# Cross-attention with chunks in twos: weighted sums of two chunks after each even chunk, two projection pieces after each odd chunk

## The chip, the cores and the metric

The kernel runs on one core of one Trainium2 chip. The metric is the device time of one execution in microseconds (us). A core has five engines that run side by side and wait for each other through semaphores: TensorE (PE, matrix products; the loading of its stationary operand is listed apart as PEld), VectorE (DVE), ScalarE (ACT), GpSimd (POOL) and SyncE (SP), which issues the transfers.

## The reference, cut to what matters

A decoder layer on 8 sequences of 512 rows and 256 features: a retention layer, a cross-attention and a mixture-of-experts layer. Only the cross-attention is touched by the change.

```python
# x: (8, 512, 256) after the retention layer, context: (8, 1601, 256), 16 heads of 16
xn = layernorm(x)
q, k, v = xn @ Wq.T + bq, context @ Wk.T + bk, context @ Wv.T + bv      # split into 16 heads
scores = einsum('bhtd,bhcd->bhtc', q, k) / sqrt(16)
out = einsum('bhtc,bhcd->bhtd', softmax(scores, axis=-1), v)
x = x + out.reshape(B, T, D) @ Wo.T + bo
```

## The kernel before, in words

The three layers follow each other. In the cross-attention, each of the 8 batches goes through 4 groups of 4 heads (`g`), and each group through 13 chunks of 128 context rows (`c`; the last has 65 rows). So a batch has 52 chunks. The programs of the engines are written out by hand; nothing reorders them. A chunk consists of these steps:

- **Scores** (line 964): four products of 128 context rows with 512 query rows, one for each head. Heads stand in pairs: one of a pair in partitions 0 to 63, the other in 64 to 127, so that a product uses half of the array's rows. The results go to three banks of PSUM in turn (`S_BANKS`), so that the fourth score of a chunk has to wait until ScalarE has taken the exponential of the first.
- **Exponentials** (line 1060, ScalarE): four per chunk, from PSUM into `x_probs`, with 8 slots before (two chunks).
- **Weighted sums** (line 948, `values`): four products of `x_probs` with the values, one for each head, each in 32 columns of the array, which accumulate over the chunks into one bank of PSUM, `PV`. In the trace each of the four shows as two records, so x8 is one chunk. They are run one chunk late. At the end of a group ScalarE copies the bank out (`evacuate`, line 1043), and the next group's first weighted sums wait for that.
- **Maxima** (line 900 on TensorE, line 1155 on VectorE; the last 66 columns are the "tails", lines 860 and 1159): the softmax subtracts each row's maximum, which has to be known before the group starts. So the scores of the next group are computed once more ahead of time, in another layout, and VectorE reduces them. About four of them belong to each chunk. Like the scores they use half of the array's rows, and a maximum and a score that stand next to each other and use different halves run together.
- **Pieces**: all other products, one after another in a table. For the next batch: 4 pieces of the projection `q` (line 879), 14 of `k` (line 886), 13 of `v` (line 893), 2 transposes `xnT` (line 873). For this one: `norm` (line 920, a group's result turned, then divided by VectorE), `oT` (line 924) and `wo` (line 931, the output projection), and `shift` (line 915, the maxima turned into rows). A `q`, `k` or `v` piece shows in the trace as x4, a `wo` piece as x8, in full array width and height. ScalarE takes `q`, `k`, `v`, `xnT`, `oT` and `shift` out of PSUM, VectorE the others.

Maxima and pieces share four banks of PSUM in turn (`W_BANKS`); each waits for what was four places ahead of it to be taken out. `woven` writes the scores of one pair of heads with the maxima around them: one maximum, the two scores, one maximum. `pieces_of` sets which piece stands in which chunk. TensorE's order in a chunk before is: two scores with two maxima, the piece (if there is one), two scores with two maxima, the weighted sums of the chunk before. In batches with a batch before and behind, 45 of 52 chunks have a piece; the seven without are chunks 0, 1 and 3 of group 0 and chunks 8, 9, 11 and 12 of group 3.

Of the kernel before, what the change touches and what calls it, by code (L numbers as in the profile page):

```python
# [23 lines left out]
P = 128  # L24
B, T, D, H = 8, 512, 256, 16
# [521 lines left out]
SPLITS = KT * NQ + KT * NK  # L547
WHOLE = 4
AHEAD = 4
NORM_CHUNK, SHIFT_CHUNK = 2, SC - 3  # L550
NEGM_AT = 320
# [24 lines left out]
def pieces_of(prev, following):  # L576

    at = [[[] for _ in range(SC)] for _ in range(G)]

    def spread(g, chunks, items):  # L580
        for c, item in zip(chunks, items):
            at[g][c].append(item)

    others = [c for c in range(SC) if c not in (NORM_CHUNK, SHIFT_CHUNK)]
    if prev:
        spread(0, (NORM_CHUNK, 4, 5, 7, 8), [("norm", G - 1), ("oT", 0), ("oT", 1), ("wo", 0), ("wo", 1)])
    for g in range(1, G):
        at[g][NORM_CHUNK].append(("norm", g - 1))
    for g in range(G):
        if g < G - 1 or following:  # L590
            at[g][SHIFT_CHUNK].append(("shift", (g + 1) % G))
    if following:
        q, k, v = q_pieces(), [k_pieces(f) for f in range(KT)], v_pieces()
        spread(0, (6, 9, 11, 12), [v[0], ("xnT", 0), ("xnT", 1), q[0]])
        spread(1, others, q[1:4] + k[0] + v[1:2])
        spread(2, others, k[1] + v[2:6])
        spread(3, others, v[6:13])
    return at


def work_of(prev, following):
# [21 lines left out]
    pieces = pieces_of(prev, following)  # L623
    return [[(first[g][c], pieces[g][c], second[g][c]) for c in range(SC)] for g in range(G)]

# [74 lines left out]
def cross_attention(nc, x_all, ln2, io, given):  # L700

    with ExitStack() as ctx:
# [21 lines left out]
        zero = sb("x_zero", [P, 1])  # L724
        probs = sb("x_probs", [P, 2 * GH, T])
        ou = sb("x_ou", [P, T])
# [127 lines left out]
        def _(pe):  # L854
# [80 lines left out]
            def values(b, g, q):  # L935

                if q == 0:
                    if b or g:
                        pe.wait_ge(pv_evac, b * G + g)
                    else:  # L940
                        pe.wait_ge(pv_zeroed, 1)
                    pe.wait_ge(v_ready, b * 2 * G + 2 * (g + 1))
                x = b * CHUNKS + g * SC + q
                pe.wait_ge(exp_done, GH * (x + 1))
                w = min(P, S - q * P)
                for j in range(GH):
                    slot = (GH * x + issued(j)) % (2 * GH)
                    m = pe.matmul(ps[32 * j:32 * j + HD + 1, PV, :], vst[g][0:w, q, j, :],  # L948
                                  probs[0:w, slot, :], start=q == 0, stop=q == SC - 1)
                m.then_inc(pv_used, 1)  # L950
# [30 lines left out]
            for b in range(B):  # L981
                for g in range(G):
                    pe.wait_ge(m_loaded, MLOADS * (b * G + g + 1))
                    for c in range(SC):
                        first, pieces, second = PLANS[b][g][c]
                        n = woven(b, g, c, 0, n, first)
                        for i in range(len(pieces)):
                            fill(b, n + i, g)
                        n = woven(b, g, c, 1, n + len(pieces), second)
                        if c:  # L990
                            values(b, g, c - 1)
                        elif b or g:
                            values(b - (g == 0), (g - 1) % G, SC - 1)
# [6 lines left out]
        def _(act):  # L1000
# [49 lines left out]
            for b in range(B):  # L1050
                for g in range(G):
                    for c in range(SC):
                        w = min(P, S - c * P)
                        for pair in range(2):
                            x = b * CHUNKS + g * SC + c
                            for s in range(GH * x + 2 * pair, GH * x + 2 * pair + 2):
                                act.wait_ge(s_filled, s + 1)
                                if x >= 2:
                                    act.wait_ge(pv_used, x - 1)
                                nc.scalar.activation(probs[0:w, s % (2 * GH), :], ps[0:w, s % S_BANKS, :],  # L1060
                                                     ACT.Exp, scale=HD ** -0.5).then_inc(exp_done, 1)
                            if c == 1 and pair == 0 and (b or g):

                                if b and g == 0:
                                    act.wait_ge(drained_v, done(b - 1, ("norm", G - 2)))
                                elif b and g == 1:
                                    act.wait_ge(drained_v, done(b, ("norm", G - 1)))
                                elif g >= 2:
                                    act.wait_ge(drained_v, done(b, ("norm", g - 2)))
                                evacuate(b * G + g)  # L1070
                            for item in [item for part in PLANS[b][g][c][2 * pair:2 * pair + 2] for item in part]:
                                if item[0] in BY_ACT:
                                    drain(b, n, g)
                                n += 1
            act.wait_ge(drained_v, done(B - 1, ("norm", G - 2)))
# [55 lines left out]
        def _(dve):  # L1131
# [75 lines left out]
            for b in range(B):  # L1207
                for g in range(G):
                    for c in range(SC):
                        if g == 0 and c == 7 and b < B - 1:  # L1210
                            dve.wait_ge(drained_a, done(b, ("oT", 1)) if b else done(LEADER, ("xnT", 1)))
                            normalise(b + 1)
# [566 lines left out]
```

## Time and profile before

| | us |
|---|---|
| median of 3 runs | 2213.64 (2205.82 to 2221.99) |
| the profiled execution, its own time | 2199.31 |
| its span, first to last instruction | 2197.5 |
| TensorE busy | 2041.6 (93%) |
| VectorE busy | 1523.5 (69%) |
| ScalarE busy | 1226.0 (56%) |
| GpSimd busy | 439.9 (20%) |

The cross-attention takes about 1330 us of the span, from some 430 us to some 1770 us. The time between two evacuations of `PV`, which are 13 chunks apart, is the period of a group. The end of a matmul in the trace is modelled, so the starts are what is read here: the distance from the start of one kind of work to the start of the next one is what the first kind costs TensorE.

### The profile page before, as it was taken

Reading aid. Unit: us, or ns where it says so; the run is one execution under the profiler, and the core shown is the slowest. Engines: PE = TensorE matmul, PEld = TensorE weight load, DVE = VectorE, ACT = ScalarE, POOL = GpSimd, SP = SyncE. Lnnn points to the kernel's source line nnn. Section 1 sums busy time; section 2 is a strip of 40 time slices with the busy share of each in tenths; the row PEclk is TensorE's granted clock in tenths of the full one; section 3 lists DMA queues with packets and bytes.
Section 4 is the critical chain, followed back from the end, with each engine's and each line's share of the span. In section 5 each row is a group of like instructions: output and inputs, shape, how many; then the busy total and the mean of one; then the engine's idle time right before and its main releaser. Section 6 shows DMA issues by size and latency. Waiting matters only on the chain. (4 is left out here: it accounts for less than half of the span.)

```text
span 2197.5 us, 36726 instructions
## 1 busy us (share of the span) xinstructions
PE 2041.6 (93%) x12946; PEld 1114.6 (51%) x12946; DVE 1523.5 (69%) x2930; ACT 1226.0 (56%) x2353; POOL 439.9 (20%) x484
## 2 busy tenths in 40 slices
PE   6898895899999999999999999999999879799999
PEld 4665664434444444444444434444433258588887
DVE  6888884677777787787787787787789266522222
ACT  2311312167767777777777777777777733222222
POOL 1100102203103112113113113112110044222222
PEclk9999997589989999999999999999999979899999
DMA  5000003434322522522521621621620010000000
GB/s 174 1 0 0 0 1 80 81 73 94 77 61 76 94 61 71 99 61 70 101 61 64 106 61 58 113 61 57 114 31 2 1 63 17 1 10 19 10 19 19
DMA packets 45373, 118.69 MB, mean 54 GB/s; under 512 B 9120, under 2 KB 21408, under 8 KB 45088
## 3 DMA queue, kind: packets, MB, share of 16 engines
q1 hardware_dynamic: 45232, 116.88, 23.7%
q8 instruction: 80, 1.31, 0.3%
q14 instruction: 61, 0.50, 0.1%
HBM read 77.30 MB, written 38.81 MB: 53 GB/s over the span
## 5 line engine op out<-in xcount | busy, mean ns | idle before, releaser
L1155 DVE TENSOR_REDUCE x_mx<-x_ps 128x1 f32<-128x512 f32 x1536 | 976.1, 685 | 217.2 <-PE x_ps L900 208.1
L1060 ACT ACTIVATE x_probs<-x_ps 128x512 f32<-128x512 f32 (+1 forms) x1664 | 894.3, 597 | 280.6 <-PE x_ps L964 274.6
L964 PE MATMUL x_ps<-x_qst,x_kst 50*128 50x512 f32 (+1 forms) x1664 | 595.6, 453 | 24.2 <-ACT x_probs L1060 22.1
L900 PE MATMUL x_ps<-x_kst,x_qst 48*128 48x512 f32 x1536 | 574.6, 462 | 16.8 <-DMA x_kst<-k_parts 11.1
L900 PEld LDWEIGHTS x_ps<-x_kst,x_qst 48*128 48x128 f32 x1536 | 240.3, 191 | 434.1 <-DVE x_mx L1155 289.2
L948 PE MATMUL x_ps<-x_probs,x_vst 128*17 128x512 f32 (+1 forms) x3328 | 446.2, 608 | 4.8 <-ACT x_ou L1043 4.8
L964 PEld LDWEIGHTS x_ps<-x_qst,x_kst 50*128 50x128 f32 (+1 forms) x1664 | 243.0, 183 | 116.4 <-ACT x_probs L1060 111.0
L1582 DVE TENSOR_TENSOR f_hid_whole<-f_ps,f_act_g 128x512 f32<-128x512 f32 x80 | 55.1, 690 | 240.8 <-PE f_ps L1339 232.2
L1454 ACT ACTIVATE f_act_g<-f_ps 128x512 f32<-128x512 f32 x80 | 47.6, 596 | 243.9 <-PE f_ps L1370 232.0
L1520 POOL TENSOR_TENSOR f_hid_rest<-f_hid_whole,f_hid_rounded 128x512 fp32r<-128x512 f32 x80 | 103.1, 1289 | 233.2 <-ACT f_hid_rounded L1460 233.2
L1092 POOL TENSOR_TENSOR x_vst<-x_v_all,x_bv 128x768 f32<-128x768 f32 x64 | 66.5, 1068 | 379.1 <-ACT x_v_all L1018 300.4
L284 ACT ACTIVATE r_qwide<-r_qT,r_headmask 128x512 f32<-128x512 f32 x128 | 80.0, 709 | 105.0 <-DVE r_qT L433 105.0
L213 PE MATMUL r_ps<-r_qwide,r_kT 128*128 128x512 f32 x256 | 116.2, 602 | 10.0 <-DVE r_vz L439 10.0
L948 PEld LDWEIGHTS x_ps<-x_probs,x_vst 128*17 128x17 f32 (+1 forms) x3328 | 55.3, 95 | 136.8 <-issue 73.3
L886 PE MATMUL x_ps<-x_ctxT,x_wk 128*128 128x256 f32 (+1 forms) x448 | 123.5, 402 | 0.0
L893 PE MATMUL x_ps<-x_wv,x_ctxT 128*128 128x256 f32 (+1 forms) x416 | 114.9, 404 | 4.0 <-DMA x_ctxT<-in_ctxT 4.0
L756 POOL TENSOR_TENSOR x_kp<-x_rest,x_zero 128x256 fp32r<-128x256 f32 (+1 forms) x105 | 59.4, 566 | 287.7 <-ACT x_rest L1038 234.4
L886 PEld LDWEIGHTS x_ps<-x_ctxT,x_wk 128*128 128x128 f32 x448 | 77.3, 197 | 45.2 <-issue 28.3
L448 DVE TENSOR_TENSOR r_probs<-r_ps,r_decay 128x512 f32<-128x512 f32 x128 | 84.5, 688 | 22.2 <-PE r_ps L213 21.4
L1384 PE MATMUL f_ps<-f_wd_rounded,f_hid_rest 128*128 128x256 f32 x320 | 91.9, 287 | 8.6 <-issue 4.6
L893 PEld LDWEIGHTS x_ps<-x_wv,x_ctxT 128*128 128x128 f32 (+1 forms) x416 | 70.3, 186 | 45.2 <-issue 25.1
L1384 PE MATMUL f_ps<-f_wd_rounded,f_hid_rounded 128*128 128x256 f32 x320 | 91.6, 286 | 0.0
(191 smaller groups left out, 2487.1 us busy)
## 6 DMA issues: line engine op xcount, KB each, us to landing
x_kst<-k_parts SPq DMA_DIRECT2D x192, 200.1 KB, 8.4
k_parts<-x_kp SPq DMA_DIRECT2D x16, 1601.0 KB, 6.0
x_ctxT<-in_ctxT SPq DMA_DIRECT2D x8, 1601.0 KB, 8.6
x_qst<-q_parts SPq DMA_DIRECT2D x192, 64.0 KB, 2.6
q_parts<-x_qp SPq DMA_DIRECT2D x8, 1024.0 KB, 4.3
x_all<-in_x SPq DMA_DIRECT2D x8, 512.0 KB, 3.9
out<-x_all SPq DMA_DIRECT2D x8, 512.0 KB, 2.9
x_qst<-x_mrows SPq DMA_DIRECT2D x128, 4.0 KB
```

The lines of the kernel that those rows point to most:

```text
L213: pe.matmul(ps[:, o, :], kT[:, f, c * P:(c + 1) * P], qwide[:, f, 4 * half:4 * half + 4, c * P:(c + 1) * P], start=True, stop=True).then_i ...
L284: ins = nc.scalar.activation(qwide[:, f, h, :], qT[:, f, :], ACT.Copy, scale=headmask[:, h:h + 1])
L448: nc.vector.tensor_tensor(probs[:, c % 2, h:h + 4, :], ps[:, item(), :].rearrange("p (h t) -> p h t", h=4), decay[:, h:h + 4, :], ALU.mult ...
L886: m = pe.matmul(o[:, 0:w], wk[:, kk, f * P:(f + 1) * P], ctxT[:, kk, c:c + w], start=kk == 0, stop=kk == KT - 1)
L893: m = pe.matmul(o[0:w, 0:D], ctxT[:, kk, c * P:c * P + w], wv[:, kk, :], start=kk == 0, stop=kk == KT - 1)
L900: m = pe.matmul(o, qst[mg][rows, pair, t * P:(t + 1) * P], kst[mg][rows, pair, i * 512:(i + 1) * 512], start=True, stop=True)
L948: m = pe.matmul(ps[32 * j:32 * j + HD + 1, PV, :], vst[g][0:w, q, j, :], probs[0:w, slot, :], start=q == 0, stop=q == SC - 1)
L964: pe.matmul(ps[0:w, n % S_BANKS, :], kst[g][rows, pair, c * P:c * P + w], qst[g][rows, pair, :], start=True, stop=True).then_inc(s_filled, 1)
L1060: nc.scalar.activation(probs[0:w, s % (2 * GH), :], ps[0:w, s % S_BANKS, :], ACT.Exp, scale=HD ** -0.5).then_inc(exp_done, 1)
L1155: nc.vector.tensor_reduce(out=mx[:, 2 * pair + half, t, i:i + 1], in_=o, axis=AX.X, op=ALU.max).then_inc(drained_v, 1)
L1384: m = pe.matmul(ps[:, DOWN + t // 2, (t % 2) * D:(t % 2 + 1) * D], hid[l][:, buf, t * P:(t + 1) * P], wd[r][:, j, :], start=start and n == ...
L1520: nc.gpsimd.tensor_tensor(hid[1][:, buf, :], hid_whole[:, buf, :], hid[0][:, buf, :], ALU.subtract).then_inc(hid_split, 1)
```

## The change

- Within a chunk all four scores now come first, with the maxima around them, and then either the piece(s) or the weighted sums, never both.
- Chunks 2, 4, ..., 12 of a group end with the weighted sums of the two chunks before them, eight products in a row. Chunk 0 ends with those of the last chunk of the group before. Odd chunks have none.
- Pieces stand in chunks 1, 3, 5, 7, 9 and 11 alone, mostly two in a row.
- `x_probs` has 12 slots in place of 8 (three chunks), `x_rest`, through which `q` and `k` pieces go to be split, has 2 in place of 4.
- ScalarE copies `PV` out after the exponentials of chunk 0 instead of in the middle of chunk 1. It takes pieces out after all four exponentials of a chunk. `normalise` for the next batch moves from chunk 7 to 5, `shift` from chunk 10 to 9, `norm` from chunk 2 to 1.

```diff
-WHOLE = 4
+WHOLE = 2
+SLOTS = 3 * GH
 AHEAD = 4
-NORM_CHUNK, SHIFT_CHUNK = 2, SC - 3
+VISITS = range(1, SC - 1, 2)
+NORM_CHUNK, SHIFT_CHUNK = VISITS[0], VISITS[4]
...
-    if following:
-        q, k, v = q_pieces(), [k_pieces(f) for f in range(KT)], v_pieces()
-        spread(0, (6, 9, 11, 12), [v[0], ("xnT", 0), ("xnT", 1), q[0]])
-        spread(1, others, q[1:4] + k[0] + v[1:2])
-        spread(2, others, k[1] + v[2:6])
-        spread(3, others, v[6:13])
...
+    if prev:
+        place(0, [("norm", G - 1)], [("oT", 0), ("oT", 1)], [("wo", 0), ("wo", 1)])
+    if following:
+        place(0, [], [], [], [("xnT", 0), ("xnT", 1)], v[0:1], q[0:2])
+        place(1, q[2:3], [q[3], k[0][0]], k[0][1:3], k[0][3:5], k[0][5:6], [k[0][6], v[1]])
+        place(2, v[2:3], k[1][0:2], k[1][2:4], k[1][4:6], k[1][6:7], v[3:5])
+        place(3, v[5:6], v[6:8], v[8:10], v[10:12], v[12:13])
...
-                        first, pieces, second = PLANS[b][g][c]
+                        first, second, pieces = PLANS[b][g][c]
                         n = woven(b, g, c, 0, n, first)
+                        n = woven(b, g, c, 1, n, second)
                         for i in range(len(pieces)):
                             fill(b, n + i, g)
-                        n = woven(b, g, c, 1, n + len(pieces), second)
-                        if c:
+                        n += len(pieces)
+                        if c and c % 2 == 0:
+                            values(b, g, c - 2)
                             values(b, g, c - 1)
-                        elif b or g:
+                        elif c == 0 and (b or g):
                             values(b - (g == 0), (g - 1) % G, SC - 1)
...
-                                if x >= 2:
-                                    act.wait_ge(pv_used, x - 1)
+                                if s >= SLOTS:
+                                    act.wait_ge(pv_used, x - SLOTS // GH + 1)
```

TensorE in group 1 of a batch, from the start of chunk 4 on, before (`kst`, `qst` are the keys and queries, `wk` and `ctxT` make a `k` piece):

```order
L900 MATMUL x_ps<-x_kst,x_qst 128x512
L964 MATMUL x_ps<-x_qst,x_kst 128x512 x2
L900 MATMUL x_ps<-x_kst,x_qst 128x512
L886 MATMUL x_ps<-x_ctxT,x_wk 128x256 x2
L900 MATMUL x_ps<-x_kst,x_qst 128x512
L964 MATMUL x_ps<-x_qst,x_kst 128x512 x2
L900 MATMUL x_ps<-x_kst,x_qst 128x512
L948 MATMUL x_ps<-x_probs,x_vst 17x512 x4
L900 MATMUL x_ps<-x_kst,x_qst 128x512
L964 MATMUL x_ps<-x_qst,x_kst 128x512 x2
L900 MATMUL x_ps<-x_kst,x_qst 128x512
L886 MATMUL x_ps<-x_ctxT,x_wk 128x256 x2
```

The same place in the changed kernel, where line numbers are one higher (900 is 901, 964 is 965, 948 is 949, 886 is 887):

```order
L901 MATMUL x_ps<-x_kst,x_qst 128x512
L965 MATMUL x_ps<-x_qst,x_kst 128x512 x2
L901 MATMUL x_ps<-x_kst,x_qst 128x512 x2
L965 MATMUL x_ps<-x_qst,x_kst 128x512 x2
L901 MATMUL x_ps<-x_kst,x_qst 128x512
L949 MATMUL x_ps<-x_probs,x_vst 17x512 x8
L901 MATMUL x_ps<-x_kst,x_qst 128x512
L965 MATMUL x_ps<-x_qst,x_kst 128x512 x2
L901 MATMUL x_ps<-x_kst,x_qst 128x512 x2
L965 MATMUL x_ps<-x_qst,x_kst 128x512 x2
L901 MATMUL x_ps<-x_kst,x_qst 128x512
L887 MATMUL x_ps<-x_ctxT,x_wk 128x256 x4
```

The piece has left the place between the two halves of the scores; the weighted sums come for two chunks at once, and two `k` pieces in a row. Over the whole program, TensorE's unbroken stretches of scores and maxima go from 744 to 398, those of weighted sums from 415 to 223, those of pieces from 331 to 177. The products themselves are the same.

ScalarE around the change from one group to the next in batch 0, before (65x512 is chunk 12; `x_ou` is the evacuation, `x_v_all` a `v` piece taken out):

```order
L1060 ACTIVATE x_probs<-x_ps 65x512 x2
L1060 ACTIVATE x_probs<-x_ps 128x512 x2
L1018 ACTIVATE x_v_all<-x_ps 128x256
L1060 ACTIVATE x_probs<-x_ps 128x512 x4
L1043 ACTIVATE x_ou<-x_ps 128x512
L1018 ACTIVATE x_v_all<-x_ps 128x256
```

The same place in the changed kernel (lines are three higher):

```order
L1063 ACTIVATE x_probs<-x_ps 65x512 x4
L1063 ACTIVATE x_probs<-x_ps 128x512 x4
L1046 ACTIVATE x_ou<-x_ps 128x512
L1063 ACTIVATE x_probs<-x_ps 128x512 x4
L1021 ACTIVATE x_v_all<-x_ps 128x256
```

The evacuation now stands behind the four exponentials of chunk 0, before any of chunk 1; the piece is taken out once all four of chunk 1 are done.

## Rows read from the trace of the kernel before

**Rows 1.** The page's first part: each engine's busy time and share.

```profile
PE 2041.6 (93%) x12946; PEld 1114.6 (51%) x12946; DVE 1523.5 (69%) x2930; ACT 1226.0 (56%) x2353; POOL 439.9 (20%) x484
```

**Rows 2.** Windows from evacuation to evacuation: batch 2 group 1, 3; then batch 3, 7, 1.

```profile
core 0: us, PE busy (x) PEld busy (x) DVE busy (x) ACT busy (x) POOL busy (x), PEclk, DMA share, GB/s
828.45:870.95 42.50, 42.50 (x274) 18.27 (x272) 33.38 (x58) 32.99 (x67) 11.99 (x19) 1.00 0.17 65
...
913.44:952.86 39.42, 37.95 (x254) 15.24 (x252) 33.05 (x58) 30.56 (x62) 7.59 (x7) 1.00 0.39 82
952.86:994.71 41.85, 41.12 (x274) 18.01 (x272) 35.57 (x64) 31.52 (x63) 3.42 (x6) 1.00 0.20 31
1660.02:1695.58 35.56, 32.37 (x230) 12.16 (x228) 32.48 (x58) 27.85 (x55) 0.00 (x0) 1.00 0.01 2
614.80:662.16 47.36, 46.89 (x274) 20.03 (x272) 35.78 (x64) 31.63 (x62) 3.43 (x6) 0.86 0.20 27
```

**Rows 3.** Timeline of TensorE: start, length; a chunk with a piece.

```profile
745.61 0.50 PE L900 MATMUL x_ps<-x_kst,x_qst 48*128 48x512 f32 x1
...
746.28 1.13 PE L893 MATMUL x_ps<-x_wv,x_ctxT 128*128 128x256 f32 x4
747.34 0.49 PE L900 MATMUL x_ps<-x_kst,x_qst 48*128 48x512 f32 x1
...
748.00 1.05 PE L948 MATMUL x_ps<-x_probs,x_vst 128*17 128x512 f32 x8
748.99 0.50 PE L964 MATMUL x_ps<-x_qst,x_kst 50*128 50x512 f32 x2
...
749.79 0.66 PE L920 MATMUL x_ps<-x_ident,x_ou 128*128 128x128 f32 x4
```

**Rows 4.** Timeline of TensorE and two others: a chunk without a piece.

```profile
1650.60 0.49 PE L900 MATMUL x_ps<-x_kst,x_qst 48*128 48x512 f32 x1
...
1650.93 0.39 PE L900 MATMUL x_ps<-x_kst,x_qst 48*128 48x512 f32 x1
...
1651.13 2.48 DVE L1155 TENSOR_REDUCE x_mx<-x_ps 128x1 f32<-128x512 f32 x4 [0.20 <-PE x_ps L900]
1651.16 2.06 ACT L1060 ACTIVATE x_probs<-x_ps 128x512 f32<-128x512 f32 x4 [0.20 <-PE x_ps L964]
1651.16 0.39 PE L964 MATMUL x_ps<-x_qst,x_kst 50*128 50x512 f32 x1
...
1651.81 0.49 PE L964 MATMUL x_ps<-x_qst,x_kst 50*128 50x512 f32 x1 [0.26 <-ACT x_probs L1060]
...
1652.24 1.05 PE L948 MATMUL x_ps<-x_probs,x_vst 128*17 128x512 f32 x8
...
1653.22 0.50 PE L900 MATMUL x_ps<-x_kst,x_qst 48*128 48x512 f32 x1
```

**Rows 5.** The page: the line of the weighted sums; busy, then mean ns.

```profile
L948 PE MATMUL x_ps<-x_probs,x_vst 128*17 128x512 f32 (+1 forms) x3328 | 446.2, 608 | 4.8 <-ACT x_ou L1043 4.8
```

**Rows 6.** Timeline of TensorE: a `wo` piece, eight products in a row.

```profile
803.72 1.99 PE L931 MATMUL x_ps<-x_wo,x_oT 128*128 128x256 f32 x8
805.64 0.50 PE L900 MATMUL x_ps<-x_kst,x_qst 48*128 48x512 f32 x1
```

**Rows 7.** Timeline of TensorE: tails at a chunk's end, no piece in it.

```profile
768.85 0.49 PE L900 MATMUL x_ps<-x_kst,x_qst 48*128 48x512 f32 x1
...
770.16 0.76 PE L860 MATMUL x_ps<-x_kst,x_qst 48*128 48x66 f32 x8
770.85 1.05 PE L948 MATMUL x_ps<-x_probs,x_vst 128*17 128x512 f32 x8
```

**Rows 8.** Timeline of TensorE: a wait for the evacuation, chunk 1 of group 0.

```profile
786.25 0.50 PE L964 MATMUL x_ps<-x_qst,x_kst 50*128 50x512 f32 x1 [0.25 <-ACT x_probs L1060]
...
787.22 1.05 PE L948 MATMUL x_ps<-x_probs,x_vst 128*17 128x512 f32 x8 [0.47 <-ACT x_ou L1043]
```

**Rows 9.** Timeline of TensorE: the wait for the context in batch 0.

```profile
461.39 2.05 PE L893 MATMUL x_ps<-x_wv,x_ctxT 128*128 128x256 f32 x4 [3.99 <-DMA x_ctxT<-in_ctxT]
```

More of the change, by code:

```diff
@@ L578, in pieces_of, with place @@
     at = [[[] for _ in range(SC)] for _ in range(G)]
[L580 to L584, printed above, removed]
+    def place(g, *visits):
+        for c, items in zip(VISITS, visits):
+            at[g][c] += items
+    q, k, v = q_pieces(), [k_pieces(f) for f in range(KT)], v_pieces()
     if prev:
-        spread(0, (NORM_CHUNK, 4, 5, 7, 8), [("norm", G - 1), ("oT", 0), ("oT", 1), ("wo", 0), ("wo", 1)])
-    for g in range(1, G):
-        at[g][NORM_CHUNK].append(("norm", g - 1))
+        place(0, [("norm", G - 1)], [("oT", 0), ("oT", 1)], [("wo", 0), ("wo", 1)])
[4 more added lines that the diff above has]
+        place(3, v[5:6], v[6:8], v[8:10], v[10:12], v[12:13])
     for g in range(G):
+        if g:
+            at[g][NORM_CHUNK].append(("norm", g - 1))
         if g < G - 1 or following:
             at[g][SHIFT_CHUNK].append(("shift", (g + 1) % G))
-    if following:
-        q, k, v = q_pieces(), [k_pieces(f) for f in range(KT)], v_pieces()
-        spread(0, (6, 9, 11, 12), [v[0], ("xnT", 0), ("xnT", 1), q[0]])
-        spread(1, others, q[1:4] + k[0] + v[1:2])
-        spread(2, others, k[1] + v[2:6])
-        spread(3, others, v[6:13])
     return at
@@ L623, in work_of @@
     pieces = pieces_of(prev, following)
-    return [[(first[g][c], pieces[g][c], second[g][c]) for c in range(SC)] for g in range(G)]
+    return [[(first[g][c], second[g][c], pieces[g][c]) for c in range(SC)] for g in range(G)]
 def order(plan):
@@ L724, in cross_attention @@
         zero = sb("x_zero", [P, 1])
-        probs = sb("x_probs", [P, 2 * GH, T])
+        probs = sb("x_probs", [P, SLOTS, T])
         ou = sb("x_ou", [P, T])
@@ L946, in values @@
                 for j in range(GH):
-                    slot = (GH * x + issued(j)) % (2 * GH)
+                    slot = (GH * x + issued(j)) % SLOTS
                     m = pe.matmul(ps[32 * j:32 * j + HD + 1, PV, :], vst[g][0:w, q, j, :],
@@ L1209, in _ @@
                     for c in range(SC):
-                        if g == 0 and c == 7 and b < B - 1:
+                        if g == 0 and c == 5 and b < B - 1:
                             dve.wait_ge(drained_a, done(b, ("oT", 1)) if b else done(LEADER, ("xnT", 1)))
```

26 lines of the change are left out of this document (13 added, 13 removed).

## The prediction

> **What bounds the kernel now.** I read the page's shares first. TensorE is busy for 93% of the span, VectorE for 69%, ScalarE for 56% [rows 1]. A share says little on its own, so the second view is windows cut at the evacuations of `PV`, one per group. In group 1 of batch 2 (828.45 to 870.95) TensorE is busy for 42.50 of 42.50 us, VectorE for 33.38 and ScalarE for 32.99; only where chunks without pieces lie does TensorE show some idle time, 1.5 us in group 3 [rows 2]. So TensorE bounds the cross-attention, and its neighbours have about a fifth to spare. The evacuations of a steady batch are 42.50, 42.49, 39.42 and 41.85 us apart, 166.3 us in all [rows 2]; the left-out row between 870.95 and 913.44 is the 42.49 of group 2.
>
> The third view is the timeline, read by starts. A chunk with a piece is four stretches: scores and maxima 0.67 us (745.61 to 746.28), piece 1.06, scores and maxima 0.66, weighted sums 0.98 to 0.99; 3.38 us together [rows 3]. A chunk without a piece is two: scores and maxima 1.64 us (1650.60 to 1652.24), weighted sums 0.98; 2.62 us [rows 4]. Look at what the 1.64 consists of. The first pair of products takes 0.33, the next 0.23, but the fourth starts 1.21 us after the first, not 0.8: it waits for ScalarE (0.26 us idle), since the fourth score needs the bank of the first, whose exponential began only at 1651.16. With a piece in the middle this wait does not show, because the piece takes longer than the wait. Two halves with something between them cost 0.67 + 0.66 = 1.33 us; the same products in one stretch cost 1.64.
>
> I checked that these prices add up. A steady batch has 38 chunks of the plain split kind (1.33), 7 split ones with tails in them (0.67 + 0.80, the 0.80 from 748.99 to 749.79 [rows 3]), 6 whole ones (1.64), one whole one with tails (768.85 to 770.85, 2.00 [rows 7]), a wait for the evacuation (787.22 - 786.25 = 0.97 in place of 0.43, so 0.54 [rows 8]), 52 weighted sums at 0.98 and 45 pieces: 73.2 + 51.0 + 41.8 = 166.0 us, against 166.3. The sizes of the pieces are 1.06 for `q`, `k`, `v`, 1.92 for `wo` [rows 6], 0.59 for a transpose (from 749.79 to 750.37 in the same timeline), 0.34 for `shift`. Nothing else waits in a steady batch.
>
> **The change, part by part, for one steady batch.**
>
> *Scores and maxima.* All 52 chunks now have them in one stretch, and nothing is put between the first and the fourth score. That is word for word the order of the chunks without a piece, so I take their price: 1.64 [rows 4], 2.00 where the tails come last [rows 7]; where the tails come first, in chunk 2, 1.64, since they fall into the wait. 38 x (1.64 - 1.33) = +11.8; four chunks with tails first, 1.64 - 1.47 each = +0.7; three with tails last, 2.00 - 1.47 = +1.6; the evacuation's 0.54 goes, as the first weighted sums of a group now come at the end of chunk 2. Together +13.5 us (11.8 + 0.7 + 1.6 - 0.54). What bounds this from below: without any wait, four pairs in a row would cost 0.33 + 0.23 + 0.23 + 0.33 = 1.12. Nothing in the change gives a fourth bank of scores or an earlier exponential, so I take the upper value.
>
> *Weighted sums.* 24 of the 52 join the one before. The stretch of four (eight records) is 1.05 long to its modelled end and one record 0.61 [rows 4, 5], so the second half of it starts 0.44 after the first, and two such halves more cost some 0.85 to 0.88. Alone they cost 0.98. I take 0.85: -24 x 0.13 = -3.1 us. If joining gave nothing it would be 0.
>
> *Pieces.* 45 stretches become 23, so 22 pieces stand directly behind another one. Eight products in a row take 1.92 [rows 6], four 1.06 [rows 3], so the second of two costs 0.86 and joining saves 0.20. For the 9 short ones I take 0.10 to 0.15. Together -3.8 us.
>
> Sum for a steady batch: +13.5 - 3.1 - 3.8 = **+6.6 us**: 166.3 becomes 172.9. Six batches are steady: +39.
>
> Here the row of the weighted sums bears on a rule. A switch of shape costs TensorE about 0.13 us after the weighted sums, and 0.20 after a piece. The Trainium skill (TensorEngine Tiling (Array Packing), Key Properties of the Tiling Modes) says that going to another tiling mode drains TensorE, while another tile in the same mode does not. That speaks for the change, and the trace agrees that a switch costs; what it would make of the sum by itself is rival A.
>
> *The first batch.* It has no `norm`, `oT`, `wo` of a batch before, so more of its chunks are whole already: +12.4 - 3.3 - 3.4 = +5.7. But its first `v` piece waits 3.99 us for the context, and takes 2.05 in place of 1.13 right after, since the clock has gone to half [rows 9]. The piece moves from chunk 6 to chunk 9, some 9 us later, so the wait goes, and about 3 us of slow clock with it: -7. Net -1.
>
> *The last batch.* Nearly all its chunks are whole already, at 35.56 us a group [rows 2]. Now two chunks stand between weighted sums: 1.64 + 1.64 + 1.83 = 5.11 in place of 5.24, if nothing waits. But VectorE needs 2.48 us for four maxima [rows 4], 4.96 for eight, with TensorE asking for them unevenly, 3.5 us apart and then 1.6. So the gain is eaten, and I expect -0.1 to +0.3 us for each two chunks; with the few split chunks it loses, +2 us (-2 to +6).
>
> *Costed at nothing.* The 12 slots: the weighted sums that free a slot stand ahead on TensorE of the scores that need it. `x_rest` with 2 places: two pieces come 0.9 us apart, the next two 7 us later; GpSimd is busy for 12 of 42.5 us [rows 2]. ScalarE's evacuation behind chunk 0: it ends about when the first score of chunk 1 is there; it can cost 0.1 us a group. The four banks of maxima and pieces: with 3.5 us for a chunk and 2.48 for its maxima [rows 4] each is taken out before its turn. If this cover were gone, 0.2 us for each of 23 visits would be 5 us a batch.
>
> *The clock.* One group, the one from 614.80, takes 47.36 instead of 41.85 us, at a mean clock of 0.86 instead of 1.00 [rows 2]: 5.5 us for one fall to the lower level (1.2 of 2.4 GHz). It comes where chunks 8 to 12, 0 and 1 follow each other with one piece among them, and TensorE waits 0.26 us in each of the others. The same stretch two batches on, ahead of 952.86, was followed by a clock of 1.00. With the change only chunk 11 of group 3 has neither a piece nor weighted sums, so the work is more even, and I take this fall as gone: -5.5.
>
> Against the profiled execution: 39 - 1 + 2 - 5.5 = +35, so 2199.3 becomes 2234. The median run is 14.3 us longer than the profiled one, as much as 2.6 more of such falls. I can't see where it is lost; if it is such falls, some go too. I take 3 us off: 2213.6 + 35 - 3 = **2246 us**, 1.4% slower.
>
> **The rivals.**
>
> *A, the switches decide.* TensorE's stretches in the cross-attention fall by nearly half. If the wait for the exponential did not come back, the scores of a chunk would cost 1.12 instead of 1.33: -10 us a batch for scores, -6.9 for the rest, some -130 us in all, 2085 us. For it: weighted sums and pieces do get cheaper in a row. Against it: every whole chunk in the trace has the 0.26 us wait. It would need ScalarE's first exponential 0.5 us earlier. Chance 0.04.
>
> *B, the clock gives it back: not slower.* If the median run has 3 to 4 falls at 5.5 us each and the change removes all, that is -20 from a raw sum of +40: 2234, within 1%. For it: the spread of the runs (2206 to 2222) is three such steps. To come out even it needs 7 falls; below 3 the forecast stands. Chance 0.23.
>
> *C, more falls or no gain from joining.* If the 0.26 us of waiting in every chunk halves the clock at each of the seven batch borders, +33; if the weighted sums in a row cost 0.98 each, +25. Either gives 2270 to 2287. Against it: whole chunks in batch 7 run at clock 1.00 [rows 2]. Chance 0.08.
>
> **How the numbers follow.** The forecast, 2236 to 2262, has 0.65; it is bounded below by one or two more falls gone and above by the last batch at +6, no fall gone and a loss of 0.1 us a visit. Slower than that is C. The range that leaves out 2 in 10 reaches down into B: 2225 to 2263. Under 1% (22 us) this kernel's runs can't tell a change from none. Slower by over 1%: 0.65 + 0.08 = 0.73; within 1%: B, 0.23; faster: A, 0.04.
>
> **What would show it.** Windows between evacuations: groups 1 and 2 of a steady batch go from 42.5 to 43.7, group 3 from 39.4 to 42.2, group 0 from 41.9 to 43.2. In the timeline of TensorE, each chunk's scores start with a first pair and a fourth 1.2 us later, idle for ScalarE, ahead of 1.83 us of weighted sums or 1.92 us of pieces. The idle time of TensorE ahead of line 965 for ScalarE comes to some 400 x 0.26 = 104 us. The wait for the context in batch 0 is gone. I am wrong if a stretch of four pairs is under 1.5 us, if eight weighted sums take 1.96, or if the mean clock of the cross-attention changes by more than 0.02.

## The result: 3.4% slower

| | before | changed |
|---|---|---|
| median of 4 runs, us | 2216.71 (2205.82 to 2221.99) | 2288.07 (2282.76 to 2301.98) |
| ratio, 95% interval | | 1.034 (1.028 to 1.040) |
| the profiled execution, us | 2199.31 | 2287.74 |

2246 us was forecast, +32; it became +71, above the range's end of 2263. So the direction was right and the size less than half. The two traces, cut at the same three evacuations (that of the last group of batch 0, that of the last group of batch 6, and the last of all), show where the 88 us between the two profiled executions lie. The columns are the window, its length, the busy times of the five rows of engines (PE, PEld, DVE, ACT, POOL), and TensorE's granted clock (third from the right). The kernel before:

```profile
0.00:614.80 614.80, 524.07 (x3464) 313.10 (x3464) 470.28 (x1073) 233.74 (x445) 96.94 (x111) 0.92 0.23 55
614.80:1617.88 1003.08, 990.11 (x6410) 420.70 (x6408) 812.38 (x1405) 768.20 (x1507) 200.63 (x271) 0.99 0.35 75
1617.88:1764.77 146.89, 132.43 (x838) 47.35 (x836) 86.45 (x154) 109.11 (x212) 0.74 (x2) 0.95 0.06 8
1764.77:2197.50 432.73, 394.97 (x2238) 333.46 (x2238) 154.36 (x300) 114.95 (x192) 141.54 (x102) 0.95 0.06 20
```

The changed kernel:

```profile
0.00:625.38 625.38, 529.60 (x3458) 322.72 (x3460) 466.80 (x1071) 229.95 (x443) 95.58 (x111) 0.91 0.23 55
625.38:1682.80 1057.42, 983.03 (x6410) 469.84 (x6410) 796.79 (x1405) 747.44 (x1507) 200.72 (x271) 0.99 0.33 71
1682.80:1849.30 166.50, 155.98 (x844) 57.83 (x842) 85.93 (x156) 107.58 (x213) 2.08 (x2) 0.87 0.05 7
1849.30:2286.00 436.70, 398.07 (x2206) 335.57 (x2238) 154.83 (x300) 114.78 (x192) 141.41 (x102) 0.95 0.06 20
```

| part | forecast | measured |
|---|---|---|
| up to the evacuation of batch 0's last group | -1 | +10.6 |
| six batches | +39, less 5.5 for the clock | +54.3 |
| last batch | +2 | +19.6, clock 0.95 to 0.87 |
| behind the cross-attention | 0 | +4.0 |

Look at the second row of each: TensorE's busy time fell by 7 us while the window grew by 54. TensorE is still the engine all others wait for, but it now stands idle itself. The groups of a steady batch, the answer to [rows 2]:

```profile
977.00:1021.15 44.15, 40.80 (x274) 20.04 (x274) 35.01 (x64) 30.64 (x62) 4.77 (x6) 1.00 0.14 20
1021.15:1065.29 44.14, 40.87 (x270) 19.61 (x270) 32.60 (x58) 31.77 (x64) 11.36 (x18) 1.00 0.16 62
1065.29:1109.49 44.20, 41.16 (x270) 19.76 (x270) 32.62 (x58) 31.49 (x64) 11.06 (x15) 1.00 0.65 126
1109.49:1152.24 42.75, 39.78 (x262) 18.59 (x262) 32.53 (x58) 30.60 (x63) 6.24 (x7) 1.00 0.36 77
```

43.2, 43.7, 43.7 and 42.2 were forecast for groups 0 to 3. A steady batch without a fall of the clock takes 175.0 us, 8.7 more than the 166.3 of [rows 2], where 6.6 had been worked out. Measured from start to start, such a batch (1152.24 to 1327.25) is 88.8 us of scores and maxima, 48.1 of weighted sums and 38.1 of pieces. In the kernel before it is 73.4, 51.1 and 41.8. So scores and maxima cost 15.4 us more (13.5 forecast), and the joined blocks give back 3.0 and 3.65 (3.1 and 3.8 forecast).

Why TensorE is idle shows in the timeline, which answers to [rows 3, 4]; first an even, then an odd chunk:

```profile
1031.22 0.50 PE L901 MATMUL x_ps<-x_kst,x_qst 48*128 48x512 f32 x1
...
1032.44 0.50 PE L965 MATMUL x_ps<-x_qst,x_kst 50*128 50x512 f32 x1 [0.25 <-ACT x_probs L1063]
...
1032.87 1.91 PE L949 MATMUL x_ps<-x_probs,x_vst 128*17 128x512 f32 x16
1034.71 0.49 PE L901 MATMUL x_ps<-x_kst,x_qst 48*128 48x512 f32 x1
...
1035.92 0.49 PE L965 MATMUL x_ps<-x_qst,x_kst 50*128 50x512 f32 x1 [0.24 <-ACT x_probs L1063]
...
1036.36 2.00 PE L887 MATMUL x_ps<-x_ctxT,x_wk 128*128 128x256 f32 x8
1038.28 0.50 PE L901 MATMUL x_ps<-x_kst,x_qst 48*128 48x512 f32 x1
```

The stretch of scores takes 1.65 us, the fourth score comes 1.22 us after the first and TensorE waits 0.25 us for its bank; then 1.84 us for eight weighted sums and 1.92 for two pieces. These were forecast as 1.64, 1.21, 0.26, 1.83 and 1.92. On the page the wait shows as the idle time ahead of line 965 (964 before), 92.1 us for ScalarE where it was 22.1 and 104 was forecast; first the kernel before, then the changed one:

```profile
L964 PE MATMUL x_ps<-x_qst,x_kst 50*128 50x512 f32 (+1 forms) x1664 | 595.6, 453 | 24.2 <-ACT x_probs L1060 22.1
L965 PE MATMUL x_ps<-x_qst,x_kst 50*128 50x512 f32 (+1 forms) x1664 | 626.9, 457 | 95.0 <-ACT x_probs L1063 92.1
```

### The profile page after: what moved, and what is told of

The parts are those of the page before. It is cut to its first block and busy times, and to the rows that moved or that the text cites. A ratio compares the mean times of both kernels' runs of the same rounds, so it can differ in the third digit from the quotient of the medians.

```text
span 2286.0 us, 36692 instructions
## 1 busy us (share of the span) xinstructions
PE 2066.7 (90%) x12914; PEld 1186.0 (52%) x12946; DVE 1504.4 (66%) x2930; ACT 1199.7 (52%) x2353; POOL 439.8 (19%) x484
## 5 line engine op out<-in xcount | busy, mean ns | idle before, releaser
L1157 DVE TENSOR_REDUCE x_mx<-x_ps 128x1 f32<-128x512 f32 x1536 | 953.9, 683 | 324.9 <-PE x_ps L901 321.0
L1063 ACT ACTIVATE x_probs<-x_ps 128x512 f32<-128x512 f32 (+1 forms) x1664 | 855.4, 604 | 364.6 <-PE x_ps L965 360.5
L965 PE MATMUL x_ps<-x_qst,x_kst 50*128 50x512 f32 (+1 forms) x1664 | 626.9, 457 | 95.0 <-ACT x_probs L1063 92.1
L901 PE MATMUL x_ps<-x_kst,x_qst 48*128 48x512 f32 x1536 | 585.5, 468 | 17.2 <-DMA x_kst<-k_parts 11.3
L949 PE MATMUL x_ps<-x_probs,x_vst 128*17 128x512 f32 (+1 forms) x3328 | 426.8, 630 | 0.0
L965 PEld LDWEIGHTS x_ps<-x_qst,x_kst 50*128 50x128 f32 (+1 forms) x1664 | 270.7, 184 | 300.1 <-ACT x_probs L1063 283.0
L901 PEld LDWEIGHTS x_ps<-x_kst,x_qst 48*128 48x128 f32 x1536 | 262.5, 192 | 279.9 <-DVE x_mx L1157 150.1
L949 PEld LDWEIGHTS x_ps<-x_probs,x_vst 128*17 128x17 f32 (+1 forms) x3328 | 77.1, 99 | 185.5 <-issue 124.0
L887 PE MATMUL x_ps<-x_ctxT,x_wk 128*128 128x256 f32 (+1 forms) x448 | 113.4, 393 | 0.0
L1386 PE MATMUL f_ps<-f_wd_rest,f_hid_rounded 128*128 128x256 f32 x320 | 91.8, 287 | 0.0
```

What stands on the lines that cost most here:

```text
L887: m = pe.matmul(o[:, 0:w], wk[:, kk, f * P:(f + 1) * P], ctxT[:, kk, c:c + w], start=kk == 0, stop=kk == KT - 1)
L901: m = pe.matmul(o, qst[mg][rows, pair, t * P:(t + 1) * P], kst[mg][rows, pair, i * 512:(i + 1) * 512], start=True, stop=True)
L965: pe.matmul(ps[0:w, n % S_BANKS, :], kst[g][rows, pair, c * P:c * P + w], qst[g][rows, pair, :], start=True, stop=True).then_inc(s_filled, 1)
L1063: nc.scalar.activation(probs[0:w, s % SLOTS, :], ps[0:w, s % S_BANKS, :], ACT.Exp, scale=HD ** -0.5).then_inc(exp_done, 1)
L1157: nc.vector.tensor_reduce(out=mx[:, 2 * pair + half, t, i:i + 1], in_=o, axis=AX.X, op=ALU.max).then_inc(drained_v, 1)
L1386: m = pe.matmul(ps[:, DOWN + t // 2, (t % 2) * D:(t % 2 + 1) * D], hid[l][:, buf, t * P:(t + 1) * P], wd[r][:, j, :], start=start and n == ...
```

## The experiments

Two questions: is it really the bank of scores, rather than the places of the pieces or the joined blocks themselves, and what is the clock's part? Each kernel was timed beside the kernel before on the same chip, whose median was 2206.78 to 2211.32 us; only the ratio of the changed kernel is to the 2216.71 us of the result.

| kernel | us | ratio to before (95%) | a steady batch, us | last batch, us |
|---|---|---|---|---|
| before | 2211 | | 166.3 | 146.9 |
| changed | 2288 | 1.034 (1.028 to 1.040) | 175.0 | 166.5 |
| late: piece behind the scores, nothing joined | 2297 | 1.041 (1.034 to 1.048) | 180.4 | 145.8 |
| mid: joined work between the score pairs | 2303 | 1.041 (1.036 to 1.046) | 177.4 | 173.4 |
| val2: weighted sums joined alone | 2296 | 1.037 (1.032 to 1.041) | 176.6 | 177.4 |
| pc2: pieces joined alone | 2281 | 1.029 (1.022 to 1.036) | 174.2 | 173.1 |
| half_before: half exponentials | 2181 | 0.985 (0.980 to 0.989) | 164.6 | 131.6 |
| half_after: the same, changed kernel | 2187 | 0.987 (0.982 to 0.992) | 164.8 | 143.7 |
| s4_before: 4 + 3 banks | 2253 | 1.018 (1.013 to 1.023) | 171.7 | 139.5 |
| s4_after: 4 + 3 banks | 2364 | 1.068 (1.063 to 1.073) | 184.2 | 174.9 |
| unjoin: no stretch of eight scores | 2287 | 1.033 (1.029 to 1.038) | 174.9 | 169.1 |
| pad: idle products in the last batch | 2291 | 1.036 (1.031 to 1.042) | 175.0 | 161.3 |

The times of batches are distances between evacuations in the trace of each kernel; the steady one is the commonest of the six, or one without a fall of the clock (in `mid` and `pc2` 3.4 us at half clock belong to it in every batch, in `val2` 6.8, in `s4_after` 3.4). `before2`, `after2`, `unjoin2` and `spread3` had one execution each, told below. The cuts of the edits show TensorE's part; what ScalarE does otherwise is told beside them.

**late**, the order alone.

```diff
-    return [[(first[g][c], pieces[g][c], second[g][c]) ...
+    return [[(first[g][c], second[g][c], pieces[g][c]) ...
         n = woven(b, g, c, 0, n, first)
-        for i in range(len(pieces)): fill(b, n + i, g)
-        n = woven(b, g, c, 1, n + len(pieces), second)
+        n = woven(b, g, c, 1, n, second)
+        for i in range(len(pieces)): fill(b, n + i, g)
+        n += len(pieces)
```

> The kernel before with one edit: in each chunk the piece stands behind all four scores, directly ahead of the weighted sums; nothing is joined. Bank theory: 45 chunks a batch pay 0.31 us more for the scores, with tails a bit more, some +13 us a batch and +100 in all, 2315. If instead the joined blocks themselves starve the other engines (rival), this kernel stays nearer to the one before, under 2260.

It came to +86 us in all, 2297, against the +100 expected and well above the 2260 of the rival. A steady batch costs 14.1 us more, where 13.5 had been worked out for this term of the change (and "some +13" here). Nothing is joined; besides the order on TensorE, ScalarE takes a piece out after all four exponentials of its chunk, as in the changed kernel. A steady batch of the changed kernel is 180.4 - 175.0 = 5.4 us shorter than this one, where 6.9 had been forecast for the joins. The joined blocks do give back 6.7 us; 1.3 are lost again in stretches of scores that are a little longer (88.8 against 87.5 us). Its last batch, in which nearly all chunks were whole before, is as long as before. The groups of batch 2, in windows:

```profile
855.38:902.04 46.66, 43.63 (x274) 19.31 (x272) 32.51 (x58) 32.46 (x66) 12.54 (x20) 1.00 0.15 61
902.04:948.64 46.60, 43.67 (x274) 19.34 (x272) 32.51 (x58) 32.11 (x67) 9.89 (x14) 1.00 0.61 114
```

TensorE, with the same products, is idle for 3 of 46.6 us; in [rows 2] for none of 42.5.

**mid**, the joined work in the middle.

```diff
         n = woven(b, g, c, 0, n, first)
-        n = woven(b, g, c, 1, n, second)
         for i in range(len(pieces)): fill(b, n + i, g)
         n += len(pieces)
...
+        n = woven(b, g, c, 1, n, second)
```

(ScalarE takes pieces out after each pair's exponentials again, as in the kernel before.)

> The changed kernel, but the joined work (two pieces, or the weighted sums of two chunks) stands between the two halves of a chunk's scores, as the piece did before. Bank theory: with one gap per chunk there are still four scores between two gaps (second half of a chunk and first half of the next), and the fourth still waits for the bank of the first. So stretches of scores stay at 1.64 us and the time within 10 us of the changed kernel, 2288. Place theory (the rival: the cost comes from the piece having left the middle of the chunk): stretches of 0.67 us come back, about 56 us less than the kernel before, 2160.

The place theory falls. TensorE's timeline has the same stretch of 1.65 us with the same wait, now made of the second half of one chunk and the first of the next:

```profile
904.25 0.49 PE L901 MATMUL x_ps<-x_kst,x_qst 48*128 48x512 f32 x1
...
905.46 0.50 PE L965 MATMUL x_ps<-x_qst,x_kst 50*128 50x512 f32 x1 [0.24 <-ACT x_probs L1063]
...
905.89 1.99 PE L887 MATMUL x_ps<-x_ctxT,x_wk 128*128 128x256 f32 x8
```

What counts is not where the gaps are but how many: one gap per chunk means four scores per stretch, wherever it is put. The kernel is 15 us slower than the changed one, more than the 10 allowed for. Its steady batches have 3.4 us at half clock each and its last one 58 of 173.4.

**val2 and pc2**, one join each.

```diff
 # val2: before, with SLOTS = 3 * GH, WHOLE = 2, and
-        if c: values(b, g, c - 1)
+        if c and c % 2 == 0: values(b, g, c - 2); values(b, g, c - 1)
 # pc2: before, with pieces_of of the changed kernel (two pieces in odd chunks, still in the middle)
```

> The kernel before with the weighted sums of two chunks at the end of even chunks, 12 slots, pieces one by one in the middle as before. Bank theory: between an odd and an even chunk nothing separates four scores, so 26 stretches a batch go from twice 0.67 to 1.64, +8, and the joining gives back 3: +5 a batch, +40, 2256. If the joining is a gain without a price (rival), -24: 2192.

> The kernel before with the other join alone: pieces in twos in the middle of odd chunks, weighted sums of one chunk at each chunk's end. Bank theory: all even chunks now have four scores in one stretch, 22 more than before in a steady batch, +6.8 us; joining pieces gives back 3.8: +3 us a batch, and a little in the first, +24 in all: 2236. If joining is a gain without a price (rival), -28: 2183.

Both are slower than before, so neither join is a gain without a price; but they lose twice and three times what was worked out (+85 and +70 us against +40 and +24). For `pc2` 3 us a steady batch had been expected and 7.9 came (some 1.5 of it from 3.4 us at half clock). I had counted only stretches of four, but in these two kernels gaps are uneven: `val2` has four stretches of six scores a batch between an odd chunk without a piece and the next, some 2.6 us each (3.0 to 3.7 with tails), and both have a last batch of over 170 us, of which 68 (`val2`) and 75 us (`pc2`) ran at half clock. The sums for them were too simple; only their sign carries weight.

**half_after and half_before**, a shorter wait.

```diff
-  activation(probs[0:w, s % SLOTS, :], ps[0:w, s % S_BANKS, :], Exp, ...)
+  activation(probs[0:w, s % SLOTS, 0:T // 2], ps[0:w, s % S_BANKS, 0:T // 2], Exp, ...)
```

> The changed kernel with exponentials of only 256 of the 512 query columns (the other half of the probabilities is left at one, so half of the output is not the reference's). Bank theory: the fourth score waits for a shorter exponential, about 1.0 us after the first instead of 1.21, so each stretch of four scores falls from 1.65 to about 1.43 us, 11 us a batch, 90 in all: 2195. If the wait is not what costs (rival), nothing changes: 2285.

> The kernel before with the same cut of the exponentials. Bank theory: only the stretches of four gain, 7 in a steady batch and most in the last, 0.2 us each, some 17 us: 2195. The distance between the two kernels, 75 us with whole exponentials, is then under 15 us. By the rival it stays at 75.

This pair decides. TensorE's work is the same to the last product; only the exponentials are shorter (all of them, and GpSimd sets `x_probs` to one at the start). The distance between the kernels shrinks from 71 to 6 us. In the steady batches, where no fall of the clock blurs it, the 8.7 us between 175.0 and 166.3 become 0.2 between 164.8 and 164.6. Both kernels came out faster than the 2195 expected. In the last batch, where most chunks are whole, `half_before` gains 15.3 us and none of it is at half clock any more. The timeline of `half_after`, the stretch now 1.43 us and no wait shown ahead of a product:

```profile
835.90 0.49 PE L901 MATMUL x_ps<-x_kst,x_qst 48*128 48x512 f32 x1
...
836.48 0.92 PE L965 MATMUL x_ps<-x_qst,x_kst 50*128 50x512 f32 x2
836.91 0.50 PE L901 MATMUL x_ps<-x_kst,x_qst 48*128 48x512 f32 x1
837.33 1.99 PE L887 MATMUL x_ps<-x_ctxT,x_wk 128*128 128x256 f32 x8
```

1.43 us is still more than the 1.12 of a stretch without any wait: the loading of the fourth score's operand (PEld) still waits 0.47 us for ScalarE. So rival A had a point: with ScalarE some 0.2 us earlier the two arrangements are level, and with 0.5 us, the figure given there, the joined one might win, which was not tried. As all exponentials are shorter, this pair alone can't tell the wait for the bank from ScalarE's load as a whole; the next pair can.

**s4_after and s4_before**, another bank.

```diff
-W_BANKS = 4
-S_BANKS = 3
+W_BANKS = 3
+S_BANKS = 4
```

> The changed kernel with four banks for scores and three for maxima and pieces in place of three and four. Bank theory: the fourth score no longer waits for ScalarE, but the fourth maximum of a stretch now waits for the bank of the first, which VectorE frees about 1.3 us after the first started, so the stretch stays at about 1.7 us and only the releaser's name changes: 2290 to 2320. If VectorE's bank is free in time, stretches fall to 1.12 us and the time to about 2080.

> The kernel before with four banks for scores and three for maxima and pieces. The split stretches have a gap of a microsecond between their halves, so neither kind of bank should be waited for there: within 15 us of the kernel before, 2211. If three banks are too few for maxima and a piece together, each piece adds a wait of 0.2 to 0.5 us, and it is slower by 60 to 150 us.

With a fourth bank for scores and whole exponentials, the wait for ScalarE ahead of the scores is gone, 2.3 us in the whole run where the changed kernel has 92.1:

```profile
L965 PE MATMUL x_ps<-x_qst,x_kst 50*128 50x512 f32 (+1 forms) x1664 | 529.8, 439 | 2.7 <-ACT x_probs L1063 2.3
```

But the bank taken from the maxima is missed at once. The fourth maximum now starts 1.27 us after the first, and the stretch takes 1.70 us ahead of weighted sums and 1.88 ahead of pieces:

```profile
929.38 0.49 PE L901 MATMUL x_ps<-x_kst,x_qst 48*128 48x512 f32 x1
...
930.65 0.50 PE L901 MATMUL x_ps<-x_kst,x_qst 48*128 48x512 f32 x1
931.08 1.91 PE L949 MATMUL x_ps<-x_probs,x_vst 128*17 128x512 f32 x16
932.92 0.50 PE L901 MATMUL x_ps<-x_kst,x_qst 48*128 48x512 f32 x1
...
934.20 0.50 PE L901 MATMUL x_ps<-x_kst,x_qst 48*128 48x512 f32 x1
934.80 1.99 PE L887 MATMUL x_ps<-x_ctxT,x_wk 128*128 128x256 f32 x8
```

2364 us is beyond the 2290 to 2320 expected: the pieces were left out of that sum, which start late too. In the kernel before the exchange costs 5.4 us a steady batch and 42 us in all (2253), between the two cases written down. The seven banks that this kernel has beside `PV` are not enough for four scores and four maxima in one stretch, whichever way they are shared out here.

**unjoin, pad, after2, before2, unjoin2, spread3**, the clock.

```diff
 # unjoin: the changed kernel; an odd chunk without pieces ends with the weighted sums of one chunk
+        if c % 2 and not pieces:
+            values(b, g, c - 1)
 # pad: the changed kernel; each odd chunk of the last batch without a piece gets an idle one
+        matmul(o[:, 0:D], ctxT[:, kk, 0:P], wv[:, kk, :])          # kk = 0, 1
 # spread3: the changed kernel; a piece in chunk 11 of group 3
-        place(3, v[5:6], v[6:8], v[8:10], v[10:12], v[12:13])
+        place(3, v[5:6], v[6:8], v[8:10], v[10:11], v[11:12], v[12:13])
```

> The changed kernel, but an odd chunk without pieces ends with the weighted sums of the chunk before, so that no stretch holds eight scores; the next even chunk then has only one chunk's. Clock theory: the falls of the clock at the end of group 3 and in the last batch come from those stretches of eight; the last batch goes from 166 us (between its evacuations) to about 150, and some 3 us at each of the other ends of group 3 go too: 2265, mean clock 0.96. If the falls have another cause, only 0.3 us per such stretch goes, some 8 us: 2280, mean clock unchanged at 0.95.

> The changed kernel with more work: in the last batch each of the 15 odd chunks that have no piece gets one idle product of the size of a v piece (its result is taken out and used by nobody). At full clock the last batch should take 15 x (3.62 + 1.84) + 9 pairs with pieces at 5.9 + 4 x 2.6 and the wo pieces, about 148 us, without the idle products, and 159 us with them. Clock theory: stretches of eight scores are what makes the clock fall in the last batch (166.5 us, 44 of them at half clock); with the products in between it stays up, and the last batch is shorter than 166.5 in spite of the added work: about 160, and the whole near 2282. If the falls don't depend on it (rival), the added 16 us come on top: 2304.

> The changed kernel once more, for a second trace. If the falls of the clock belong to the kernel's rhythm, they stand at the same places (ends of group 3, last batch) and the last batch takes 160 us or more again; if they are chance, it may be near 148.

> The kernel before once more, for a second trace. The steady batches should again take 166.3 us. If its falls of the clock are chance, the last batch (146.9) and the start of batch 1 (5.5 us lost) differ this time; the kernel's spread of runs is then the clock's.

> The kernel without stretches of eight scores once more, for a second trace. If its long fall in the last group was chance, the last batch now takes about 147 us, as in the kernel before, whose chunks look the same there; if it belongs to the rhythm, about 169 again, with some 70 us at half clock.

> The changed kernel with the last v piece moved from chunk 9 to chunk 11 of group 3, and the one before it alone in chunk 9, so that chunks 11 and 12 no longer have their eight scores in one stretch in batches 0 to 6. Clock theory: the falls at the ends of group 3 (3.4 or 6.8 us at half clock in three of six steady batches in each trace) go, group 3 stays at 42.8 us or 0.3 us less, all six steady batches take 174.5 to 175.5. If the falls have another cause, three of the six stay at 176.6 to 178.

In the last batch 15 of the 24 odd chunks have no piece, so the scores of two chunks follow each other, eight in a stretch of some 3.6 us, and then come eight weighted sums. In the changed kernel 44 of this batch's 166.5 us ran at half clock (by the granted clock, twice 0.13 of the window), in its second execution (`after2`) 55 of 169.2; in the kernel before 14 of 146.9, and again 14 of 146.8 (`before2`). Eight weighted sums that begin at half clock take 3.06 us here by starts (1824.67 to 1827.73), and 3.55 where all of it is at half clock, in place of 1.84:

```profile
1821.99 2.75 PE L965 MATMUL x_ps<-x_qst,x_kst 50*128 50x512 f32 x5 [0.45 <-ACT x_probs L1063]
1824.67 3.13 PE L949 MATMUL x_ps<-x_probs,x_vst 128*17 128x512 f32 x16
1827.73 0.73 PE L965 MATMUL x_ps<-x_qst,x_kst 50*128 50x512 f32 x3
```

`pad` adds 15 products of 1.06 us and the last batch gets shorter, at a clock of 0.98:

```profile
1682.93:1844.20 161.27, 145.70 (x904) 61.17 (x902) 86.79 (x156) 111.51 (x228) 2.10 (x2) 0.98 0.05 6
```

161.3 less the added 16 us, and with 15 stretches of eight costing 0.3 us more each than two of four, is 150 us at nearly full clock. So of the last batch's 19.6 us, the falls are some 16, by this estimate. The whole kernel did not get faster by it: its median, 2291, lies between the 2282 and 2304 written down and within the spread of the changed kernel's runs (2283 to 2302).

But my explanation, that the stretches of eight are what pulls the clock down, falls. `unjoin` has none of them behind the first two chunks of batch 0. It came to 2287 us, neither the 2265 of the clock theory nor the 2280 of its rival, and its last batch took 169.1 us (167.6 in `unjoin2`), 68 and 61 of them at half clock. Its last group, which has no maxima, ran at half clock from end to end. The last group of `late`, with the same eleven stretches of four scores, ran at full clock; first `unjoin`, then `late`:

```profile
1794.40:1845.30 50.90, 47.65 (x156) 11.98 (x156) 0.68 (x2) 25.49 (x50) 0.00 (x0) 0.50 0.00 0
1830.50:1862.40 31.90, 26.30 (x153) 7.25 (x152) 0.68 (x2) 24.31 (x48) 0.00 (x0) 1.00 0.00 1
```

`unjoin2` has 0.53 for the same group (1795.9 to 1845.6). In `pc2`, whose last group differs from `late`'s only in the place of one piece (`norm`), it took 49.7 us, 47.8 of them at half clock; the kernel before recovers there after 6.8 us. And `spread3` (2284 us), which has no stretch of eight in batches 1 to 6, still fell in four of these six (3.4 to 6.8 us each; 174.9 to 177.7 us a batch).

How far do falls come back? The long ones of the last batch do, in both executions of the kernel before, of the changed kernel and of `unjoin`. The short ones of the steady batches only in part: the changed kernel has them in batches 2, 5 and 6, `after2` in 2, 4, 5 and 6, mostly at other places. The kernel before lost 5.5 us in batch 1 alone; `before2` lost 3.0 us in batch 1 and 3.0 in batch 4, which took 169.2 us instead of the 166.3 expected. Which feature of the order decides is open. A wait in every chunk is not enough: `late` has it in all batches, and its last batch has 3.4 us at half clock.

## Why the prediction was wrong

**The mechanism was right, and shown.** The wait of the fourth score for the bank of the first is what the change brings to all chunks. `late` prices it at 14.1 us a batch by itself, and `mid` shows that it follows the number of gaps. With a fourth bank (`s4_after`) the wait for ScalarE is gone, and shortening the exponentials takes 65 of the 71 us away. None of the signs of being wrong that the prediction names came about: the mean clock of the cross-attention went from 0.98 to 0.97.

**What is missing from the sum.** 2234 us was forecast for the profiled execution and 2287.7 measured. Of the 54 us between them, 13.4 are the steady batches' scores and joins, 7.4 the clock in these six batches (5.5 forecast as gained, 1.9 lost), 17.6 the last batch, 11.6 the first and 4.0 the rest. So the clock and the first batch, which were forecast as gains, weigh more than the mis-sized term of the steady batch.

**The steady batch: the term for scores and maxima was mis-sized by a seventh.** +6.6 us was worked out, +8.7 measured; over six batches 13 us. The term itself is +15.4 where +13.5 was forecast. What was too low is the stretch of four, taken at 1.64 throughout. Measured by starts, at full clock, it is 1.64 to 1.65 behind `q`, `k`, `v` and `wo` pieces, but 1.74 in the median behind `shift` (24 of them), 1.77 in chunk 1, behind the evacuation, and 1.92 behind `oT`. ScalarE is still taking these out, so the exponential that frees the bank begins later. Here it starts 0.77 us after the first score, not 0.56, and the fourth score 1.48 us after it, not 1.21:

```profile
1160.50 1.12 ACT L1029 ACTIVATE x_oT<-x_ps 128x512 f32<-128x512 f32 x2
...
1160.68 0.74 PE L965 MATMUL x_ps<-x_qst,x_kst 50*128 50x512 f32 x2
...
1161.45 2.13 ACT L1063 ACTIVATE x_probs<-x_ps 128x512 f32<-128x512 f32 x4
...
1162.16 0.50 PE L965 MATMUL x_ps<-x_qst,x_kst 50*128 50x512 f32 x1 [0.36 <-ACT x_probs L1063]
...
1162.59 0.62 PE L949 MATMUL x_ps<-x_probs,x_vst 128*17 128x512 f32 x4
```

The prediction had 0.1 us a group for the evacuation, and nothing for the others. Two more kinds are longer: tails behind `xnT` take 2.28 us, not 2.00, and the one stretch of eight, of chunks 11 and 12 of group 3, takes 3.6, not 2 x 1.64.

**The switches.** Eight weighted sums in a row cost 1.84 us, 0.12 less than twice four. The Trainium skill (TensorEngine Tiling (Array Packing), Key Properties of the Tiling Modes) says that a change of tiling mode drains TensorE. The trace agrees in so far as a change costs these 0.12 us; whether they are a drain it doesn't show. The 6.7 us a batch that all joined blocks give back are less than half of the 15.4 that the longer stretches of scores take.

**The last batch: failed.** The step "so the gain is eaten, and I expect -0.1 to +0.3 us for each two chunks" was right in the part on engines: 3.60 + 1.84 = 5.44 us at full clock against 5.24. It left the clock out. The measured +19.6 is mostly clock (some 16 by `pad`).

**The clock: failed, with its sign.** "The work is more even, and I take this fall as gone: -5.5", and 3 more off for the median. The fall at the start of batch 1 did become shorter (3.4 us at half clock, not 13.7), but others came in three of the six steady batches, and 31 us more of half clock in the last one. Rival C, more falls, had the right sign and a chance of 0.08. That 2288 us lies at the end of its 2270 to 2287 is luck: the rival had falls at every batch border, but most of the added half clock came in the last batch. Its condition, "the 0.26 us of waiting in every chunk", does not explain them, as `late` shows. Rival B, to which 0.23 went, was the wrong way round. I took a clock of 1.00 in one group of batch 7 as evidence that whole chunks don't pull the clock down, although that batch as a whole already had 0.95. The 14 us by which the median run was longer than the profiled one, which I couldn't place, may well be clock: beside the experiments, the kernel's longest runs (2223 to 2225 us) have a mean clock of 0.950 over the whole program, its shortest (2201 to 2207) 0.960 to 0.965.

**The first batch: failed.** "The wait goes, and about 3 us of slow clock with it: -7". The wait for the context went, but the seven microseconds were not saved. The batch has seven chunks without a piece at its start, so it too has stretches of eight, and it has falls: two of 6.8 us at half clock in group 0, where there was one, and 6.8 us more behind it, where there was none. From the first score to the first evacuation it took 57.5 us instead of 57.0, although the wait was gone. The three groups behind that took 9.7 us more; 6.7 of these are what the same groups of a steady batch lose, the other 3 are the falls.

**The rest** (+4.0) lies behind the cross-attention, where no product was changed; the two executions of the kernel before differ by 2.8 us there, so it is not evidence.

## What to carry to other kernels

Joining work of one kind saves switches (0.12 us for weighted sums, 0.20 for a piece here), but it also takes away gaps, and it is the gaps that hide the latency of a ring of PSUM banks (banks used in turn). Count how many products of the ring stand between two gaps before and after: with three banks and 1.2 us from a score's start to its bank's release, three in a row are free and the fourth costs 0.3 us. Look also at what else the freeing engine has to do between two stretches, since it delays the first release. And look at the mean clock of every stretch, not of one: here the clock took some 16 of the 20 us lost in the last batch, and these runs give no rule for where it falls.

## What the runs showed of the hardware that was not expected

- The granted clock of the changed kernel fell to half in stretches in which TensorE, by the records, was not idle for more than some 0.6 us at once. In the last group of `unjoin` it stayed at half for all of the 50 us, and in a second execution for nearly all (0.53). `late`, with the same stretches of scores there, kept full clock, and the group took 31.9 us instead of 50.9.
- Falls come back in part from one execution of a kernel to the next: in the changed kernel two in the first batch, one at 1328.8 and 1329.0 us and the first of the last batch (1707.7 and 1707.8 us) at the same place, others not.
- 15 additional products of 1.06 us made a batch 5.2 us shorter (166.5 to 161.3) in the profiled execution, with a clock of 0.98 instead of 0.87.
- Switching costs TensorE as much as was read off: eight weighted sums in a row take 1.84 us, four 0.98; 16 products of `wo` in a row 3.65 us, eight 1.92.
